# Residual rows stored early and gated rows added by GpSimd's transfers, with GpSimd's row transfers released by each step's product

## The reference, cut to what matters

```
xn  = layernorm(x)
s   = state-space block(xn)      # a recurrence over the tokens, then a gate
g   = silu(feed-forward(xn))     # abel path + 2 of 8 experts per token, mixed by a gate
out = x + s * g
```

## Time and profile before

| | |
|---|---|
| median of 3 runs | 480.06 us (479.4 to 481.37) |
| the profiled execution | 482.13 us |
| its span, first to last instruction | 480.3 us |
| mean granted TensorE clock | 0.859 of 2.4 GHz |
| busy: TensorE, VectorE, ScalarE, GpSimd | 362.2, 297.9, 202.9, 149.3 us |
| GpSimd's 128 row transfers | 122.6 us of issue |
| moved by DMA | 54.34 MB, mean 113 GB/s |

### The profile page before, as it was taken

The page is one execution under the profiler, slowest core; times in us unless marked ns, Lnnn a source line. Parts: engine busy times, 40 slices in busy tenths (PEclk is TensorE's granted clock), DMA queues, the critical chain, the costliest instruction groups (busy, mean ns, idle before and its releaser), DMA issues.

```text
span 480.3 us, 11929 instructions
## 1 busy us (share of the span) xinstructions
PE 362.2 (75%) x4219; PEld 255.4 (53%) x4219; DVE 297.9 (62%) x1380; ACT 202.9 (42%) x577; POOL 149.3 (31%) x187
## 2 busy tenths in 40 slices
PE   2748798928988898879999597788679766768740
PEld 2638666625555556657687475476367422224430
DVE  3985469615555556668776355757667534566993
ACT  1138824003232225446475456376574523445310
POOL 5050001554344334440000443434000344552233
PEclk9969959869778879999999889779897959899965
DMA  8197000210003005836748468158324211111112
GB/s 277 29 292 227 2 0 3 102 64 33 33 28 104 33 23 184 277 112 233 235 156 276 142 182 249 44 175 264 88 100 151 62 39 34 34 35 25 45 47 89
DMA packets 52680, 54.34 MB, mean 113 GB/s; under 512 B 6649, under 2 KB 38560, under 8 KB 52640
## 3 DMA queue, kind: packets, MB, share of 16 engines
q1 hardware_dynamic: 37695, 38.21, 23.7%
q0 software_dynamic: 4096, 8.43, 6.5%
q10 hardware_dynamic: 10848, 7.25, 4.9%
HBM read 14.11 MB, written 16.56 MB: 64 GB/s over the span
## 4 chain that ended last, share of the span: by engine, by line
PE 49%; DVE 28%; ACT 8%; issue 6%; another core or an unknown queue 4%; DMA 2%; SPq 0%; DVEq 0%; ACTq 0%
PE bank L1082 21%; PE bank L364 5%; PE bank L1431 4%; DVE wT L974 4%; DVE xpad L1222 4%; DVE ring L986 4%; PE bank L1440 3%; PE bank L1404 2%; PE bank L1413 1%; ACT desk L1534 1%; ACT xpad L1265 1%; PE bank L1397 1%; DVE late L986 1%; PE bank L423 1%
## 5 line engine op out<-in xcount | busy, mean ns | idle before, releaser
L1082 PE MATMUL bank<-Mrep,wT 32*32 32x64 f32 x2560 | 74.7, 234 | 58.5 <-DVE wT L974 53.6
L1082 PEld LDWEIGHTS bank<-Mrep,wT 32*32 32x32 f32 x2560 | 49.2, 111 | 117.5 <-issue 116.9
L1672 POOL DMA_INDIRECT pulls<-expert_rows,slots x64 | 61.1, 955 | 159.1 <-DVE ring L986 83.2
L1658 POOL DMA_INDIRECT sorted_rows<-late,slots x64 | 61.5, 961 | 76.4 <-DVE ring L986 57.3
L986 DVE SCALAR_TENSOR_TENSOR ring<-bank,Rho,Dv 128x64 f32<-128x64 f32 x124 | 35.2, 284 | 76.3 <-PE bank L1082 69.8
L1534 ACT ACTIVATE desk<-bank,record 128x128 f32<-128x128 f32 x156 | 48.5, 362 | 59.4 <-PE bank L1431 54.2
L1431 PE MATMUL bank<-desk,record 128*128 128x128 f32 x312 | 59.2, 315 | 0.4 <-DMA record<-experts 0.4
L1440 PE MATMUL bank<-record,desk 128*128 128x129 f32 x312 | 51.8, 291 | 8.0 <-ACT desk L1534 8.0
L364 PE MATMUL bank<-bias,ones 128*128 128x512 bf16 x165 | 56.1, 448 | 0.0
L1440 PEld LDWEIGHTS bank<-record,desk 128*128 128x128 f32 x312 | 44.1, 204 | 9.5 <-issue 9.2
L1431 PEld LDWEIGHTS bank<-desk,record 128*128 128x128 f32 x312 | 43.6, 202 | 8.3 <-issue 1.4
(11 more groups left out here) (318 smaller groups left out, 625.7 us busy)
## 6 DMA issues: line engine op xcount, KB each, us to landing
record<-experts SPq DMA_DIRECT2D x78, 290.5 KB
sorted_rows<-zero_rows SPq DMA_DIRECT2D x2, 2496.0 KB, 16.8
expert_rows<-rows_out ACTq DMA_DIRECT2D x12, 322.5 KB
desk<-sorted_rows SPq DMA_DIRECT2D x12, 320.0 KB
X<-in_L_attn_x ACTq DMA_DIRECT2D x4, 512.0 KB, 6.6
out<-experts SPq DMA_DIRECT2D x8, 256.0 KB, 2.1
expert_rows<-rows_out ACTq DMA_DIRECT2D x6, 193.5 KB
desk<-sorted_rows SPq DMA_DIRECT2D x6, 192.0 KB
```

The costliest lines, as they stand in the source:

```text
L1082: t = pe.matmul(psY[q], wT[q, 32 * c:32 * c + 32], Mrep[q, c, :], start=(c == 0), stop=(c == 1))
L1658: pool.indirect_dma_start(sorted_rows[h], bass.IndirectOffsetOnAxis(ap=slots[:, j, q:q + 1], axis=0), z_rows[:, q, :], None)\
L1672: pool.indirect_dma_start(pulls[:, n % 3, j, s, :], None, expert_rows[n // (NB // HALVES)], bass.IndirectOffsetOnAxis(ap=slots[:, j, q:q + ...
```

## The change

It does three things. `UNPACED` goes from 10 to 5. The paced scatters and all gathers wait for `product` in place of `state`, with the same count. In the last part, SyncE writes the input rows `X` to the output as soon as its queue is free, with no wait; GpSimd waits for these eight stores and then, batch by batch, issues a transfer that adds `outb` onto the output in memory. The eight sums on GpSimd and VectorE are gone.

```diff
-        UNPACED = 10
+        UNPACED = 5
...
         def gated_ssm(dve, again, n):
             dve.wait_ge(sem("ssm"), NB * again + n + 1)
             dve.scalar_tensor_tensor(out=outb[:, n], in0=banks[4 + n % 4][:, :].rearrange("p (s h) -> p s h", s=SUB), scalar=0.25,
                                      in1=gates[:, n], op0=ALU.mult, op1=ALU.mult).then_inc(sem("gated_ssm"), 1)
-            if n == NB - 1:
-                dve.wait_ge(sem("gated_ssm"), NB * again + n + 1)
-                dve.tensor_tensor(outb[:, n], outb[:, n], X[:, n * SUB:(n + 1) * SUB, :], ALU.add).then_inc(sem("last_rows"), 1)
...
+        out_rows = out.rearrange("b (q k) h -> (b q) k h", k=L)
+
+        def residual_rows(sp, again):
+            if again:
+                sp.wait_ge(sem("out_stored"), 16 * NB)
+            for n in range(NB):
+                sp.dma_start(out_rows[:, n * SUB:(n + 1) * SUB, :], X[:, n * SUB:(n + 1) * SUB, :]).then_inc(sem("residual"), 16)
+
         def pool_tail(pool, again):
-            for n in range(NB - 1):
+            pool.wait_ge(sem("residual"), 16 * NB * (again + 1))
+            for n in range(NB):
                 pool.wait_ge(sem("gated_ssm"), NB * again + n + 1)
-                pool.tensor_tensor(outb[:, n], outb[:, n], X[:, n * SUB:(n + 1) * SUB, :], ALU.add).then_inc(sem("summed_rows"), 1)
-
-        def store_tail(sp, again):
-            out_rows = out.rearrange("b (q k) h -> (b q) k h", k=L)
-            for n in range(NB):
-                if n < NB - 1:
-                    sp.wait_ge(sem("summed_rows"), (NB - 1) * again + n + 1)
-                else:
-                    sp.wait_ge(sem("last_rows"), again + 1)
-                sp.dma_start(out_rows[:, n * SUB:(n + 1) * SUB, :], outb[:, n]).then_inc(sem("out_stored"), 16)
+                pool.dma_start(out_rows[:, n * SUB:(n + 1) * SUB, :], outb[:, n], accum_op=ALU.add).then_inc(sem("out_stored"), 16)
             if again:
-                sp.wait_ge(sem("out_stored"), 16 * NB * 2)
+                pool.wait_ge(sem("out_stored"), 16 * NB * 2)
...
                             at = (q * 2 + j) - UNPACED
                             if at >= 0:
-                                pool.wait_ge(sem("state"), scan_turn(at))
+                                pool.wait_ge(sem("product"), scan_turn(at))
...
-                            pool.wait_ge(sem("state"), scan_turn((LATE_GATHERS if n >= NB // HALVES else GATHERS) + (q % Q) * 2 + j))
+                            pool.wait_ge(sem("product"), scan_turn((LATE_GATHERS if n >= NB // HALVES else GATHERS) + (q % Q) * 2 + j))
...
-                store_tail(sp, 0)
-                fallback(sp, None, lambda eng: store_tail(eng, 1))
+                residual_rows(sp, 0)
+                fallback(sp, None, lambda eng: residual_rows(eng, 1))
                 sp.wait_ge(sem("out_stored"), 16 * NB)
```

## The result

The changed kernel takes **440.74 us** (median of 4 runs, 438.34 to 444.73) against 480.72 (4 runs) for the kernel before: ratio 0.918, 95% interval 0.909 to 0.927. The forecast was 441. Where the executions of a kernel fell into a faster and a slower group, the ratios here compare the faster ones alone, while the medians count all. The profiled execution took 438.34 us with a span of 436.5, 43.8 less than before (480.3).

The account below looks back on a forecast made before the run. The hold bounds the kernel: what TensorE finishes while GpSimd issues a row transfer reaches the others about 1.3 us after that transfer's start. Terms summed to -39.0 us, giving 441 us on the median of 480.06; range 427 to 469.

Parts of the forecast that it names:

- Unpaced scatters: Start of round 0: with UNPACED 5, step 0 is written at 96.3 in place of 104.2, -7.9 us.
- Round 0: Its 31 steps: 16 go from about 1.97 to 1.6, 15 filled by TensorE gain 0.07 each, -7.0 us.
- Round 1: 19 steps with transfers go from 2.06 to 1.62, -8.4 us; five further steps cost nothing.
- +4.0 for longer holds: Paced steps: TensorE's results come 1.6 in place of 1.3 behind one transfer in five, costing 4.0 us.
- last round: 25 steps go from 1.96 to 1.6, less 0.5 for those that had no transfer, -8.5 us.
- Bursts: Where each half's gathers begin: one transfer fewer runs ahead, -1.2 us in the first and -2.3 in the second.
- The last part: End of the kernel: no sums beside VectorE, landing 4.5 after issue, GpSimd's drain setting the end, -1.5 us.
- the hold half relieved: Rival for the paced steps: every second one stays near 1.9, time about 457 us, chance 0.16.
- the hold escaped: Rival for the last round: its steps fall to 1.26 each, time 429 us, chance 0.09.
- the fifth: Rival for the paced steps: their pace stays, only gather starts and kernel end gain, 467 us, chance 0.06.
- The slower one: Rival for the paced steps: transfers starting before `state_T` delay TensorE's matmuls, 2.15 a step, about 490 us, chance 0.12.
- The fourth rival: Late products aren't the transfers' doing, so pacing gains nothing: 478.5 us, chance 0.03; with a lossy end 480 to 482, 0.02.

Follow-up runs that it names:

- the new last part alone: Kernel before with only SyncE storing the input rows and GpSimd's transfers adding the gated rows, old pacing, UNPACED 10: 420.69 us, ratio 0.997.
- `state_T` kernel: Changed kernel with row transfers waiting for `state_T` in place of `product`: 495.2 us against 481.47 for the kernel before; 422.33 us on another chip.

## Why the prediction was right

The theory stood: a transfer's hold sets the step, and the change moves the transfer to an earlier place in the step. Most of its marks were there: step 0 at 95.7 (forecast 96.3, said about 96), transfers 0.16 behind L986 (about 0.25 behind the product, if that lands 0.1 before L986), L986 about 1.4 behind the transfer, most last-round steps at 1.60, L1231 at 0.69. Two were not: round 1's steps take 1.77, not 1.6, and GpSimd's drain ends 9.8 behind its last issue, not within 8. `state`, `product` and `state_T` are three phases of one transfer and give 2.06, 1.77 and 2.31 in round 1. The exact hit of the total is luck in part: terms that were off by up to 5.2 us, in both directions, cancel to within 0.3, as they show:

- **Unpaced scatters**, 8.5 for 7.9. The reading of the 3.08 was wrong (it is the end of a queue of eleven), the value taken near enough.
- **Round 0**, 12.2 for 7.0, the term most mis-sized. The prediction held that half of the steps are filled by TensorE at 1.85 to 1.95. They were at 1.98 and went to 1.58 to 1.69: the extra work of one step is drawn partly beside the next, so it did not fill the step; 15 steps gained 0.3 each where 0.07 was forecast. And the clock, which wasn't in the sum: before, four steps of 2.6 to 3.1 ran with a granted clock of 0.50, after it two, which is 2.9 us of the 12.2; the window's clock went from 0.81 to 0.94. Why there are two fewer isn't shown.
- **Round 1**, 5.7 for 8.4, and five further steps that lose 1.3 where nothing was taken. Where TensorE also has expert work, steps are 1.6 to 1.9 (one 2.1) and L986 comes 1.5 to 1.8 behind the transfer's start; why it is more there isn't shown. The "+4.0 for longer holds" is where the prediction put this; what round 1 (2.7), the last round (2.4) and the five steps (1.3) fell short by comes to 6.4.
- **Bursts**, 5.0 for 3.5; **last round**, 6.1 for 8.5, with five steps at 2.0 to 2.2. Three of them are those of a batch's first gather, which starts some 0.5 later in its step than the others do. Before, it began 1.04 behind L986 (once 1.33) and its step was a short one (1.74, 1.72, 1.46), with L986 0.7 or less behind that start; now it begins 0.64 behind L986 in place of 0.16, L986 follows 1.4 later, and the step takes 2.03 to 2.05. The prediction took them all as 1.6; **round 3** and **round 2** within 0.7.
- **Boundaries**: not in the sum; the one after round 0 gains with its neighbours 2.6, those after rounds 2 and 3 lose 2.0.
- **The last part**, 1.8 for 1.5. The landing took 5.7, not 4.5, and hid behind the drain, which is tied to the last issue (9.8 behind it, not 7.9).

The rivals: the hold half relieved (steps near 1.9) and the hold escaped (1.26) didn't happen, and with steps of 1.60 for 1.96 the fifth, that the pace stays, falls too. The slower one needed L1082 to start 1.4 behind a transfer; in the new phase it starts about 0.55 behind it, 0.71 behind L986. The row that it was read from, fifteen matmuls that start late, isn't the hold: the same step begins with one matmul and leaves the other fifteen for later on a chip without the hold too (the new last part alone):

```profile
361.28 0.21 PE L1082 MATMUL bank<-Mrep,wT 32*32 32x64 f32 x1
...
362.18 0.42 PE L1082 MATMUL bank<-Mrep,wT 32*32 32x64 f32 x15 [0.69 <-issue]
```

That the `state_T` kernel takes 495 where this rival said 490 is chance: there the matmuls start on time and it is their result that comes late. The fourth rival, that the transfers aren't the cause, falls with the release alone: on chips with the hold, `product` for `state` takes the kernel before from 482 to 454, and `state_T` for `product` the changed kernel from 441 to 495.

Two slips in the prediction's arithmetic change nothing in the forecast. The first rival's terms give 454 (480.06 - 15.05 - 11.4 + 2 - 1.5), not 457. And the 0.85 for "faster by more" counts the 0.02 for 480 to 482 us, which lies within 2.4 us of no change: 0.83 and 0.05.

The Trainium skill ("SBUF — State Buffer", "Who interferes with whom") says that TensorE never waits on anyone. The traces don't speak against that sentence itself: with the hold and without it L1082 starts 0.71 behind L986. The prediction drew from it that the product can't be late either, and that does not follow: without the hold L986 starts 0.12 behind the product's drawn end with a transfer beside it, with the hold 0.80 behind it. The section is about the SBUF ports; it doesn't treat when a result of TensorE reaches another engine, and it names no difference between chips of one kind.

**What stays open**: what on a chip makes the hold, and whether it is the chip's at all, since each of the five was measured on one occasion only; whether the result or only its signal is late; why about 1.4 us; why some products in the `state_T` kernel got through; and the time of the whole changed kernel on a chip without it, where its parts give ratios of 0.999, 1.003 and 0.997.

## What to carry to other kernels

When a signal comes late, measure what it is late *from*: here about 1.4 us behind the start of another engine's instruction (1.39 to 1.50 in most steps, up to 1.8 in others), in three different phases of it. Then the cure is the phase and the number of those instructions, and a queue of them must be counted with its own service time. Before tuning to such a loss, time the kernel before on more than one chip: this loss was nearly 60 us on some and nothing on others, and a change tuned to it may be worth nothing elsewhere. And look at each engine's drain at the end of a block: here GpSimd's took 8.6 to 9.6 us and the others' under 0.1, and giving the last work to VectorE and SyncE made the last part 4.2 us shorter.

## What was not expected of the hardware

- Chips differ: one kernel at 422 and 481 us, at a mean clock of about 0.91 and 0.86. It isn't the clock: round 1 is at full clock on both and takes 1.68 against 2.06 a step.
- A row transfer's hold was the same with 128 and 64 rows, and in bursts of 5, 6, 10 and 11 it comes to 1.47 to 1.53 us for each transfer.
- GpSimd's drain takes 8.6 to 9.6 us from its own start behind transfers (10.4 where it began beside its sums) and runs on for 4 to 7 us when all its transfers have landed.
- An adding transfer of 256 KB from GpSimd lands in 5.2 to 5.9 us, a plain one in 2.8.
